# Sorting edges for a graph network: ranks by compare-and-sum over row counts in place of running counts in PSUM, and fewer message sources sent in the sort

## The chip, the cores and the metric

One core of a Trainium2 chip runs the whole program as one launch. The metric is device time in microseconds (us), median of the runs. The engines: PE multiplies matrices and writes PSUM, DVE does vector work, ACT functions, POOL memsets and index-driven (indirect) DMAs, SP the plain DMAs. They are ordered only by semaphores.

## The reference

Four graph layers over 50,000 nodes of 256 values and 25,000 edges (`src`, `dst`, types, weights), each with a residual sum and a layer norm around it: a weighted sum of neighbours with a product (mean layer), a relational layer in two parts, two attention hops, and an interaction layer.

```python
x = _layernorm(x + _L0_gnn_ref(x, ..., edge_weight, src, dst))
x = _layernorm(x + _L1_gnn_ref(x, edge_index, edge_type_16, ...))
x = _layernorm(x + _L2_gnn_ref(x, ..., edge_index, edge_type_24, 2))
x = _layernorm(x + _L3_gnn_ref(x, src, dst, edge_weight, ...))
# inside a layer, for example:
agg = jax.ops.segment_sum(edge_weight[:, None] * x[edge_col], edge_row, num_segments=x.shape[0])
out = jnp.concatenate([agg, x], axis=1) @ W.T
```

The sums over neighbours need the edges grouped by node. The kernel sorts them itself, at the start: that is the part which is changed.

## The kernel before

Nodes are cut into 391 tiles of 128. An item is a group of at most 128 edges whose node lies in one tile. `sort_edges` gives each edge a place in the item lists, once by `src` (o = 0) and once by `dst` (o = 1), and one in the list of messages by relation. Edges lie as 125 partitions by 200 columns (EP, EC). The bucket of an edge is its node's tile; its rank is the seed of its bucket (128 times the bucket's first item) plus the number of edges of the bucket that come before it.

The sort goes in this order on DVE (its queue is in order, and `Chain.step` waits for each instruction):
- keys, record fields, the message places (L489 to L530), then `passed_chunks` and `chunk_kind` (L532 to L536) and a signal `s_rec` (L537) on which POOL starts to send.
- the histogram (L548 to L551): for each column and order a one-hot [125, 392] (`make`, L544) that PE adds up over all partitions with the matrix of ones into `hist` (L608). Each column waits for the ring of 8 one-hots.
- from the counts the base, end and seed of each bucket (L553 to L561), the tables of the items (`Tables.make`, L361 to L391), which SP turns through memory.
- the ranks (L566 to L590): `rank[o]` in PSUM starts as the seeds. For each column PE adds to every partition the one-hots of the partitions before it (L616, `before`); DVE reads the rank of its own edge with one compare-and-sum (L576, key equal to iota, times `rank`, summed into `rank_f`); then PE adds the rest (L626, `not_before`), and goes on to the next column. Two orders take turns. After each four columns DVE makes item and lane numbers and places (L581 to L588), and signals `s_placed`.
- `tables.number` (L592), small.

POOL sends with indirect DMAs, each of one column of 125 records or sources (`Scatter.send`, L282): the first 80 columns of sources to the message list; then per four columns, when placed, four columns of records of order 0 and two of sources (L645 to L650). It waits for the landing of each twenty when it starts the next but one. The phase ends with a barrier of all engines; `combine_weights` follows, then `mean_layer`.

`mean_layer` runs over items, a pair at a time. POOL gathers the rows of both items (L208) into a ring of 8 slots, and may gather pair p when PE is through with pair p - 4 (L223). The first 192 pairs are unrolled on POOL, and `between(pair)` (L851 to L856) sends scatters behind the gathers: 6/5 a pair, the 200 columns of records of order 1 first, then the sources that the sort has left. PE sums the gathered rows with a one-hot (L931) and multiplies (L941, L944); DVE accumulates and normalizes (L873 to L895); ACT evaluates squares, roots and the result.

## Time and profile before

| | us |
|---|---|
| runs: median (lowest, highest) of 3 | 7257.34 (7241.2, 7273.64) |
| span of the profiled execution | 7237.5 |
| PE busy, share of the span | 6315.2 (87%) |
| DVE busy | 5168.2 (71%) |
| ACT busy | 4246.8 (59%) |
| POOL busy | 3966.9 (55%) |

The page gives the span of the profiled execution, from its first to its last instruction, and no other time of it; the span lies 3.7 us below the fastest run and 19.8 us below the median. The busy shares are means over phases that differ: the sort takes the first 696 us, with ACT idle and DVE nearly full; after it PE is the busiest. A line of the page's slices shows the same: DVE at 9, 8, 8, 7 tenths in the first four slices of 181 us, ACT at 0 for three.

### The profile page before, as it was taken

The numbers are of one execution on the slowest core, as the hardware profiler recorded it, in microseconds if no ns is written. First come the engines' busy times: TensorE is split into PE (matmuls) and PEld (weight loads), VectorE is DVE, ScalarE is ACT, GpSimd is POOL, SyncE is SP. The second block draws the span as 40 slices with busy tenths as digits, with TensorE's granted clock in tenths as the row PEclk, the third lists the DMA queues.
The fourth block names the chain that finished last, engine by engine and source line by source line (L and its number), as shares of the span: only waits on it lengthen the run. The fifth ranks groups of instructions, "written<-read, shape, count | busy, mean of one in ns | idle before, by whom it ended". The sixth has DMA issues, their size and how long they took to land. (4 is left out here: it accounts for less than half of the span.)

```text
span 7237.5 us, 161640 instructions
## 1 busy us (share of the span) xinstructions
PE 6315.2 (87%) x35080; PEld 5058.0 (70%) x35081; DVE 5168.2 (71%) x17621; ACT 4246.8 (59%) x14612; POOL 3966.9 (55%) x3682
## 2 busy tenths in 40 slices
PE   5676999997789997889999888887888888899999
PEld 2222788886687776679999766665766666788888
DVE  9887788887655554247777677776666666799998
ACT  0000888885214443138888566665677777677777
POOL 6676777775636666654444444444454444444444
PEclk9555999998879998999999899999898888999999
DMA  1201666666556665557777566665566666444444
GB/s 38 6 2 37 164 189 186 183 196 187 171 153 190 191 191 174 173 177 221 220 222 220 172 200 194 191 193 177 173 199 184 189 188 181 120 125 127 127 127 120
DMA packets 1165457, 1171.57 MB, mean 162 GB/s; under 512 B 308211, under 2 KB 1039755, under 8 KB 1164574
## 3 DMA queue, kind: packets, MB, share of 16 engines
q1 hardware_dynamic: 1007326, 953.22, 43.2%
q0 software_dynamic: 158016, 217.06, 12.7%
q8 instruction: 42, 0.69, 0.0%
q14 instruction: 73, 0.60, 0.0%
HBM read 961.54 MB, written 392.35 MB: 187 GB/s over the span
## 5 line engine op out<-in xcount | busy, mean ns | idle before, releaser
L208 POOL DMA_INDIRECT landing_first<-messages,by_dst_meta x768 | 837.3, 1090 | 723.7 <-PE l1b_ps_b L1481 363.6
L208 POOL DMA_INDIRECT landing_last<-x,by_dst_meta x384 | 438.4, 1142 | 555.9 <-PE l_ps_a L1618 483.1
L1926 POOL DMA_INDIRECT landing_last<-z,by_src_meta x408 | 416.8, 1021 | 578.6 <-PE l2b_ps_g L2225 422.2
L1926 POOL DMA_INDIRECT landing_last<-x,by_src_meta x408 | 419.1, 1027 | 487.8 <-PE l2a_ps_g L2225 283.9
L208 POOL DMA_INDIRECT landing_first<-in_x,by_src_meta x384 | 403.2, 1050 | 182.2 <-issue 89.2
L944 PE MATMUL l_ps_b<-l_w,l_agg_t 128*128 128x256 f32 x1624 | 423.0, 381 | 5.4 <-issue 5.3
L1479 PE MATMUL l1b_ps_b<-root,l1b_x_t 128*128 128x256 f32 x1600 | 426.1, 389 | 0.5
L1479 PE MATMUL l1a_ps_b<-root,l1a_x_t 128*128 128x256 f32 x1584 | 417.8, 386 | 8.3 <-issue 5.7
L941 PE MATMUL l_ps_b<-l_w,l_both 128*128 128x256 f32 x1624 | 422.4, 383 | 0.2 <-issue 0.2
L917 ACT ACT_TABLE_LOAD x1 | 1.3, 1283 | 705.2 <-PEq L117 705.2
L1435 ACT ACTIVATE l1a_x_t<-l1a_ps_x,by_dst_first 128x256 f32<-128x256 f32 x400 | 167.7, 470 | 415.0 <-PE l1a_ps_x L1467 317.5
L1637 PE MATMUL l_ps_b<-l_w,l_mix_t 128*128 128x256 f32 x1592 | 396.6, 392 | 13.8 <-issue 6.1
L1387 DVE SCALAR_TENSOR_TENSOR l1a_total<-l1a_total,by_dst_keep,l1a_ps_b 128x256 f32<-128x256 f32 x394 | 186.9, 474 | 289.5 <-PE l1a_ps_b L1481 222.6
L1633 PE MATMUL l_ps_b<-l_w,l_x_t 128*128 128x256 f32 x1592 | 382.8, 384 | 2.5 <-ACT l_x_t L1598 2.5
L626 PE MATMUL sort_ps_rank<-sort_onehot,not_before 125*125 125x392 bf16 x400 | 234.8, 587 | 166.3 <-DVE sort_junk L576 145.1
L1637 PEld LDWEIGHTS l_ps_b<-l_w,l_mix_t 128*128 128x128 f32 x1592 | 286.5, 190 | 120.5 <-DVE l_mix_t L1554 72.5
L944 PEld LDWEIGHTS l_ps_b<-l_w,l_agg_t 128*128 128x128 f32 x1624 | 310.4, 191 | 51.0 <-issue 8.8
L626 PEld LDWEIGHTS sort_ps_rank<-sort_onehot,not_before 125*125 125x125 bf16 x400 | 72.0, 180 | 388.7 <-DVE sort_junk L576 336.6
L1038 POOL DMA_INDIRECT landing_first<-x,rel_index x216 | 233.8, 1082 | 165.0 <-PE ma_ps_x L1160 81.0
L1479 PEld LDWEIGHTS l1a_ps_b<-root,l1a_x_t 128*128 128x128 f32 x1584 | 286.6, 191 | 52.6 <-issue 17.6
L705 PE MATMUL l2a_ps_g<-zero_row,ones_b 128*128 128x392 bf16 x1734 | 321.5, 330 | 0.0
L941 PEld LDWEIGHTS l_ps_b<-l_w,l_both 128*128 128x128 f32 x1624 | 295.3, 192 | 33.5
(391 smaller groups left out, 20404.9 us busy)
## 6 DMA issues: line engine op xcount, KB each, us to landing
l_both<-in_x_both SPq DMA_DIRECT2D x416, 256.0 KB
l2a_x<-x SPq DMA_DIRECT2D x53, 1216.0 KB
z<-l2a_result SPq DMA_DIRECT2D x400, 152.0 KB
x<-l1b_result SPq DMA_DIRECT2D x392, 152.0 KB
l2b_x<-z SPq DMA_DIRECT2D x53, 1024.0 KB
l1b_x<-h SPq DMA_DIRECT2D x408, 128.0 KB
l1b_res<-x SPq DMA_DIRECT2D x408, 128.0 KB
l2b_res<-x SPq DMA_DIRECT2D x51, 1024.0 KB
```

The source lines that it names most:

```text
L208: pool.indirect_dma_start(gathered[:, slot, 0:D], None, source[0:count, :], bass.IndirectOffsetOnAxis(ap=rows, axis=0), bounds_check=limit ...
L626: pe.matmul(rank[o][0:EP, :], c.not_before[0:EP, 0:EP], onehot[0:EP, o, k, :], start=False, stop=True, skip_group_check=True)
L705: pe.matmul(spare, c.ones_b[:], c.zero_row[:], start=True, stop=True)
L941: pe.matmul(ps_b[k % 4], x_t[:, m, i * P:(i + 1) * P], w[:, 2 + i, :], start=(i == 0), stop=False)
L944: last = pe.matmul(ps_b[k % 4], agg_t[:, k, i * P:(i + 1) * P], w[:, i, :], start=False, stop=(i == 1))
L1038: pool.indirect_dma_start(gathered[:, slot, :], None, x_in[0:N_NODES, :], bass.IndirectOffsetOnAxis(ap=relations.index[:, chunk:chunk + 1] ...
L1387: dve.scalar_tensor_tensor(total[:, k, :], total[:, (k - 1) % RING, :], graph.keep[:, bass.ds(j, 1)], ps_b[k // 2 % 2][:, k % 2, :], ALU.m ...
L1435: act.activation(x_t[:, k, :], ps_x[k // 2 % 2][:, k % 2, :], ACT.Copy, scale=graph.first[:, bass.ds(j, 1)]).then_inc(s["xt"], 1)
L1479: pe.matmul(sums, x_t[:, k, f * P:(f + 1) * P], root[:, f, :], start=(f == 0), stop=False)
L1633: pe.matmul(ps_b[k % 4], x_t[:, k, i * P:(i + 1) * P], w1[:, i, :], start=(i == 0), stop=False)
L1637: last = pe.matmul(ps_b[k % 4], mix_t[:, k, i * P:(i + 1) * P], w2[:, i, :], start=False, stop=(i == 1))
L1926: pool.indirect_dma_start(gathered[:, k, :], None, x_in[0:N_NODES, :], bass.IndirectOffsetOnAxis(ap=rows, axis=0), bounds_check=limit, oob ...
```

## The change

- Histogram: PE multiplies the one-hots by the identity in place of the matrix of ones, so `hist[o]` holds for each partition the counts of its own row. DVE copies them to SBUF (`row_counts`); PE makes the totals from them (`total`), for base, end and seed as before.
- Offsets: PE makes for each partition the counts of all partitions before it, plus the seeds, in `hist[o]`; DVE copies them to `values[:, o, 0:392]`. Behind them `values` holds ones.
- Ranks: `keys[:, o, :]` holds 0 to 391 and behind it the buckets of the 200 columns. The rank of column c is one instruction, `find_rank`: over 392 + c elements, key equal to the column's bucket, times `values`, summed. Offsets and the earlier columns of the own row come in one sum. PE has no part in it; the one-hots of the second pass, L616 and L626 are gone. The result goes to one of four junk tiles, and an instruction waits for the fourth before it. The columns are unrolled.
- Places: in parts, spread between the ranks of the following columns (`place_part`), each four columns as before.
- Order on DVE: `tables.make` goes behind column 127; `passed_chunks`, `chunk_kind` and `relations.kind` behind the last place.
- POOL: 100 columns of sources first, then one (not two) behind each four records, so 150 in the sort. The other 50 go to the mean layer, with 250 scatters over all 192 pairs.
- Tiles are laid over others that are no longer used (`spread`, `values`, `junk`).

The old second pass (L563, L566 to L590 on DVE, L610 to L628 on PE) is taken out; its code stands above.

```diff
-SOURCES_FIRST = 80
-SOURCES_BEFORE = SOURCES_FIRST + 2 * EC // (RING // 2)
+SOURCES_FIRST = 100
+SOURCES_BEFORE = SOURCES_FIRST + EC // (RING // 2)
+SCATTERS_LATER = 2 * EC - SOURCES_BEFORE
...
-    HALF = RING // 2
+    QUAD, WIDTH, JUNKS = RING // 2, TILES + 1, 4
+    FIRST_RANKS = 128
...
+        keys = ph.sb("keys", [EP, 2, WIDTH + EC], F32)
+        values = going_on[:].rearrange("p r c -> p (r c)")[:, 0:2 * (WIDTH + EC)].rearrange("p (o c) -> p o c", o=2)
+        junk = seen[:].rearrange("p r c -> p (r c)")[:, 0:JUNKS * (WIDTH + EC)].rearrange("p (o c) -> p o c", o=JUNKS)
+        row_counts = ph.sb("row_counts", [EP, 2, WIDTH], BF16)
+        rank_f = spread[0:EP, WIDTH:WIDTH + 2 * EC].rearrange("p (o c) -> p o c", o=2)
...
+                def find_buckets():
+                    with dve.Fori(0, EC // RING) as g:
+                        for k in range(RING):
+                            dve.wait_ge(s_hist, (g * RING + k) * 2 + 2)
+                            for o in range(2):
+                                at = dve.snap(g * RING + (o * (WIDTH + EC) + WIDTH + k))
+                                dve.tensor_scalar(onehot[0:EP, o, k, :], c.iota16[0:EP, :], flat(keys)[:, bass.ds(at, 1)],
+                                                  None, ALU.is_equal).then_inc(s_hot, 1)
+
+                def find_rank(column):
+
+                    for o in range(2):
+                        n = column * 2 + o
+                        if n >= JUNKS:
+                            dve.wait_ge(s_rank, n + 1 - JUNKS)
+                        width = WIDTH + column
+                        dve.scalar_tensor_tensor(junk[:, n % JUNKS, 0:width], keys[:, o, 0:width],
+                                                 keys[:, o, width:width + 1], values[:, o, 0:width], ALU.is_equal, ALU.mult,
+                                                 accum_out=rank_f[:, o, column:column + 1]).then_inc(s_rank, 1)
+
+                def place_part(quad, part):
+
+                    at = slice(quad * QUAD, (quad + 1) * QUAD)
+                    if part == 0:
+                        dve.wait_ge(s_rank, (quad + 1) * QUAD * 2)
+                        dve.tensor_copy(rank_i[:, :, at], rank_f[:, :, at]).then_inc(s_int, 1)
+                    elif part == 1:
+                        dve.wait_ge(s_int, quad + 1)
+                        dve.tensor_single_scalar(item_i[:, :, at], rank_i[:, :, at], 7, op=ALU.logical_shift_right)\
+                            .then_inc(s_split, 1)
+                        dve.tensor_single_scalar(lane_i[:, :, at], rank_i[:, :, at], P - 1, op=ALU.bitwise_and)\
+                            .then_inc(s_split, 1)
+                    else:
+                        dve.wait_ge(s_split, quad * 2 + 2)
+                        for o in range(2):
+                            dve.scalar_tensor_tensor(place[o][:, at], lane_i[:, o, at], float(ITEMS), item_i[:, o, at],
+                                                     ALU.mult, ALU.add).then_inc(s_placed, 1)
+
+                chain.step(dve.memset(values[:, :, WIDTH:], 1.0))
+                find_buckets()
+                dve.wait_ge(s_hist, 2 * (EC + RING))
+                for o in range(2):
+                    dve.tensor_copy(row_counts[:, o, :], hist[o][0:EP, :]).then_inc(s_counts, 1)
+                for o in range(2):
+                    b = graphs[o].buckets
+
+                    dve.wait_ge(s_total, o + 1)
+                    chain.step(dve.tensor_scalar(b["int"][:], total[o][:], float(P - 1), None, ALU.add))
+                    chain.step(dve.tensor_single_scalar(b["int2"][:], b["int"][:], 7, op=ALU.logical_shift_right))
+                    chain.step(dve.tensor_scalar(b["count"][:], b["int2"][:], 1.0, None, ALU.max))
+                    chain.step(dve.tensor_tensor_scan(b["end"][:], c.ones_row[:], b["count"][:], 0.0, ALU.mult, ALU.add))
+                    chain.step(dve.tensor_tensor(b["base"][:], b["end"][:], b["count"][:], ALU.subtract))
+                    dve.tensor_scalar(b["seed"][:], b["base"][:], float(P), None, ALU.mult).then_inc(s_start, 1)
+                for o in range(2):
+                    dve.wait_ge(s_offset, o + 1)
+                    dve.tensor_copy(values[:, o, 0:WIDTH], hist[o][0:EP, :]).then_inc(s_values, 1)
+                dve.wait_ge(s_values, 2)
+                for column in range(EC):
+                    find_rank(column)
+                    quad, part = column // QUAD - 1, column % QUAD
+                    if quad >= 0 and part < 3:
+                        place_part(quad, part)
+                    if column == FIRST_RANKS - 1:
+                        tables.make(dve, c, graphs, chain)
+                        dve.drain().then_inc(s_tab, 1)
+                for part in range(3):
+                    place_part(EC // QUAD - 1, part)
...
+                            pe.matmul(hist[o][0:EP, :], c.ident_b[0:EP, 0:EP], onehot[0:EP, o, k, :], start=False, stop=True,
                                       skip_group_check=True).then_inc(s_hist, 1)
                 for o in range(2):
+                    pe.wait_ge(s_counts, o + 1)
+                    pe.matmul(total[o][:], c.ones_b[0:EP, :], row_counts[:, o, :], start=True, stop=True).then_inc(s_total, 1)
                 for o in range(2):
+                    pe.matmul(hist[o][0:EP, :], c.before[0:EP, 0:EP], row_counts[:, o, :], start=True, stop=False)
+                    pe.wait_ge(s_start, o + 1)
+                    pe.matmul(hist[o][0:EP, :], c.ones[0:1, 0:EP], graphs[o].buckets["seed"][0:1, :], start=False, stop=True)\
+                        .then_inc(s_offset, 1)
...
-                for step in range(EC // HALF):
-                    pool.wait_ge(s_placed, 2 * step + 2)
-                    for q in range(HALF):
-                        records.send(step * HALF + q)
-                    for n in (2 * step, 2 * step + 1):
-                        sources.send(SOURCES_FIRST + n)
+                for quad in range(EC // QUAD):
+                    pool.wait_ge(s_placed, 2 * quad + 2)
+                    for q in range(QUAD):
+                        records.send(quad * QUAD + q)
+                    sources.send(SOURCES_FIRST + quad)
...
+    PAIRS_FIXED = TILES // RING * PAIRS
...
-                    for n in range(pair * 6 // 5, (pair + 1) * 6 // 5):
+                    for n in range(pair * SCATTERS_LATER // PAIRS_FIXED, (pair + 1) * SCATTERS_LATER // PAIRS_FIXED):
```

## Rows read from the trace of the kernel before

**Rows 1.** Stretch, length, busy us of PE, PEld, DVE, ACT, POOL, PEclk, DMA.
```profile
62.00:167.00 105.00, 97.77 (x399) 38.40 (x399) 104.85 (x399) 0.00 (x0) 84.63 (x67) 0.98 0.07 1
167.00:201.00 34.00, 4.34 (x9) 1.57 (x8) 30.82 (x101) 0.00 (x0) 17.77 (x14) 0.58 0.05 1
201.00:691.00 490.00, 337.10 (x800) 114.75 (x800) 413.95 (x1455) 0.00 (x0) 358.32 (x300) 0.50 0.14 3
...
705.00:1643.00 938.00, 870.46 (x4501) 744.85 (x4502) 773.62 (x3151) 809.15 (x2953) 687.38 (x611) 0.98 0.67 185
```

**Rows 2.** Groups by line, POOL, 210 to 691 us: count, busy, mean, idle.
```profile
L282 POOL DMA_INDIRECT item_records<-sort_rec,sort_place x200 | 240.1, 1200 | 113.5 <-DVE dst_place L588 67.8 <-issue 45.7
L282 POOL DMA_INDIRECT rel_source_rows<-rel_source,rel_place x100 | 118.6, 1186 | 30.5 <-issue 30.5
```

**Rows 3.** Timeline of POOL in the sort: start, us, instruction, idle before.
```profile
62.25 1.44 POOL L282 DMA_INDIRECT rel_source_rows<-rel_source,rel_place  x1 [44.95 <-DVEq L537]
...
168.03 1.24 POOL L282 DMA_INDIRECT rel_source_rows<-rel_source,rel_place  x1 [0.30 <-issue]
...
209.74 1.29 POOL L282 DMA_INDIRECT item_records<-sort_rec,sort_place  x1 [21.00 <-DVE dst_place L588]
...
682.71 1.19 POOL L282 DMA_INDIRECT item_records<-sort_rec,sort_place  x1 [0.70 <-DVE dst_place L588]
...
690.17 1.18 POOL L282 DMA_INDIRECT rel_source_rows<-rel_source,rel_place  x1 [0.30 <-issue]
```

**Rows 4.** Timeline of DVE in the ranks: start us, us, instruction.
```profile
480.66 0.17 DVE L581 CAST sort_rank_i<-sort_rank_f 125x8 int32<-125x8 f32 x1
...
481.51 0.32 DVE L544 TENSOR_SCALAR sort_onehot<-iota,sort_bucket 125x392 bf16<-125x392 f16 x1
...
483.98 0.61 DVE L576 SCALAR_TENSOR_TENSOR sort_junk<-iota,sort_bucket,sort_ps_rank 125x392 f32<-125x392 f32 x1
...
484.73 0.62 DVE L576 SCALAR_TENSOR_TENSOR sort_junk<-iota,sort_bucket,sort_ps_rank 125x392 f32<-125x392 f32 x1
```

**Rows 5.** POOL beside the tables, 174 to 190 us; groups of L373 and L890.
```profile
L282 POOL DMA_INDIRECT rel_source_rows<-rel_source,rel_place x10 | 13.3, 1326 | 3.0 <-issue 3.0
...
174.91 1.18 POOL L282 DMA_INDIRECT rel_source_rows<-rel_source,rel_place  x1 [0.30 <-issue]
...
187.55 1.19 POOL L282 DMA_INDIRECT rel_source_rows<-rel_source,rel_place  x1 [0.30 <-issue]
...
L373 DVE SCALAR_TENSOR_TENSOR sort_table_junk<-iota,sort_tile_id,src_base 128x391 f32<-128x391 f32 x5 | 3.1, 626 | 0.2
...
L890 DVE SCALAR_TENSOR_TENSOR l_shifted<-l_scaled,l_inner_scale,beta 128x256 f32<-128x256 f32 x346 | 150.9, 476 | 0.0
```

**Rows 6.** Groups of DVE by line, 0 to 1300 us: the chunk kinds.
```profile
L535 DVE TENSOR_REDUCE sort_chunk_kind<-sort_passed_chunks 1x216 f32<-1x3456 f32 x1 | 3.7, 3741 | 0.0
L532 DVE TENSOR_TENSOR sort_passed_chunks<-sort_last_chunk,iota 1x3456 f32<-1x3456 f32 x1 | 3.7, 3740 | 0.0
```

**Rows 7.** Timeline of POOL in the mean layer: first gathers of some pairs.
```profile
902.67 1.04 POOL L208 DMA_INDIRECT landing_first<-in_x,by_src_meta  x1 [1.06 <-remote]
...
921.25 1.01 POOL L208 DMA_INDIRECT landing_first<-in_x,by_src_meta  x1 [1.25 <-remote]
...
926.92 1.04 POOL L208 DMA_INDIRECT landing_first<-in_x,by_src_meta  x1 [0.30 <-issue]
...
945.65 1.02 POOL L208 DMA_INDIRECT landing_first<-in_x,by_src_meta  x1 [0.30 <-issue]
...
952.11 1.04 POOL L208 DMA_INDIRECT landing_first<-in_x,by_src_meta  x1 [0.95 <-remote]
```

**Rows 8.** Timeline of PE in the mean layer, no scatters: two pairs apart.
```profile
1659.84 1.05 PE L931 MATMUL l_ps_a<-l_hot,landing_first 128*128 128x128 f32 x8
...
1668.53 1.05 PE L931 MATMUL l_ps_a<-l_hot,landing_first 128*128 128x128 f32 x8
```

**Rows 9.** Waits, 720 to 1610 us: us in total, times, longest us.
```profile
POOL landing_first L208 <- remote: 79.1, 85, 1.3
```

More of the change, by code:

```diff
@@ L350, with __init__ @@
     KEEP = 3
-    def __init__(self, ph):
+    def __init__(self, ph, junk):
         self.ints = ph.sb("ints", [P, 2, 3, ITEM_CHUNKS], I32)
@@ L457, in sort_edges @@
         s_hot, s_hist, s_start = ph.sem("hot"), ph.sem("hist"), ph.sem("start")
-        s_hot2, s_rank, s_read, s_empty = ph.sem("hot2"), ph.sem("rank"), ph.sem("read"), ph.sem("empty")
+        s_counts, s_total, s_offset, s_values = (ph.sem(n) for n in ("counts", "total", "offset", "values"))
+        s_rank, s_empty = ph.sem("rank"), ph.sem("empty")
         s_int, s_split, s_placed = ph.sem("int"), ph.sem("split"), ph.sem("placed")
@@ L462, in sort_edges @@
         s_out, s_rel = ([ph.pool_dma_sem(f"{n}{k}") for k in range(2)] for n in ("out", "rel"))
-        tables = Tables(ph)
+        tables = Tables(ph, spread)
         def flat(t):
@@ L536, in _ @@
                 dve.tensor_scalar(relations.kind[:], chunk_kind[:], float(R1 - 1), None, ALU.min)
-                dve.drain().then_inc(s_rec, 1)
-                dve.wait_ge(s_keys, 2)
-                def make(column, k, sem):
-                    for o in range(2):
-                        a = dve.snap(column + o * (EC + 1)) if not isinstance(column, int) else column + o * (EC + 1)
-                        dve.tensor_scalar(onehot[0:EP, o, k, :], c.iota16[0:EP, :], flat(bucket)[:, bass.ds(a, 1)], None,
-                                          ALU.is_equal).then_inc(sem, 1)
@@ L548, in _ @@
-                with dve.Fori(0, EC // RING) as g:
-                    for k in range(RING):
-                        dve.wait_ge(s_hist, (g * RING + k) * 2 + 2)
-                        make(g * RING + k, k, s_hot)
-                dve.wait_ge(s_hist, 2 * (EC + RING))
-                for o in range(2):
-                    b = graphs[o].buckets
-                    chain.step(dve.tensor_scalar(b["int"][:], hist[o][:], float(P - 1), None, ALU.add))
-                    chain.step(dve.tensor_single_scalar(b["int2"][:], b["int"][:], 7, op=ALU.logical_shift_right))
-                    chain.step(dve.tensor_scalar(b["count"][:], b["int2"][:], 1.0, None, ALU.max))
-                    chain.step(dve.tensor_tensor_scan(b["end"][:], c.ones_row[:], b["count"][:], 0.0, ALU.mult, ALU.add))
-                    chain.step(dve.tensor_tensor(b["base"][:], b["end"][:], b["count"][:], ALU.subtract))
-                    chain.step(dve.tensor_scalar(b["seed"][:], b["base"][:], float(P), None, ALU.mult))
```

79 lines of the change are left out of this document (17 added, 62 removed).

## The prediction

> **What bounds the kernel now.** I read the stages first: busy time of each engine stretch by stretch [rows 1]. The sort lies alone in front of everything: until its barrier no other phase runs, so each microsecond it ends earlier moves the whole rest forward. It has three stretches: the histogram (62 to 167 us, DVE 104.85 us busy of 105), the tables (167 to 201) and the ranks (201 to 691, DVE 414 and POOL 358 us busy of 490). Then comes the mean layer with its scatters (705 to about 1610), and after that nothing that the change touches.
>
> Second, who ends the ranks. POOL's groups [rows 2] and its single starts [rows 3]: after the histogram it sends, for each four columns, four records and two sources. Its waits for `dst_place` are 67.8 us in 50, of which 21.00 are the first; the steps start at 209.74 (the first) and 682.71 (the fiftieth), so one step takes 472.97 / 49 = 9.65 us. Six DMAs at 1.20 + 0.30 us are 8.97. So the ranks are bound by DVE by 0.7 us a step, with POOL close behind: whatever DVE gains above 7% is worth nothing unless POOL's list also gets shorter. This is the key to the change, for it does both.
>
> Third, the mean layer, where the taken-away sources go: there POOL issues two gathers and one or two scatters a pair, and the time of a pair depends on how many [rows 7].
>
> **Sort: DVE's side.** Before, a column costs two one-hots (L544) and two reads (L576, 0.62 us), which hand over to PE and back through semaphores [rows 4]. The change drops the second pass of one-hots, all 400 matmuls of L626 and 400 of L616, and the waits between. What is left per column is two compare-and-sum instructions from SBUF, 392 elements wide at column 0 and 591 at column 199. The trace shows the same form from SBUF in L373: 0.62 us for 391 elements, and L890 takes 476 ns for 256 [rows 5]; that is (626 - 476) / 135 = 1.11 ns an element, so the added mean width of 99.5 elements is 0.11 us. Two L576 start 0.75 us apart with their waits [rows 4]. The least that two starts can lie apart I take as 0.55 us for 392 elements, 0.626 less the 0.08 that reading an accumulator takes beside it (an estimate). So one costs 0.66 us with no wait between and 0.86 with all of them; I take 0.75, since the new one waits only for the fourth before it. 400 of them are 300 us (264 to 344). The five instructions that split ranks and make places stay; in one step they run from 480.66 to 481.51 [rows 4], 0.85 us, so 43 us; the tables, moved behind column 127, are some 25 of the 30.8 us that DVE is busy in their stretch [rows 1]. DVE then needs about 370 us for the ranks (332 to 412), where it has 490 now.
>
> Before that come small new things: a memset and the copies of row counts, two matmuls of totals, two pairs of offset matmuls and two copies, some 5 us by my estimate, all while POOL is still sending its first hundred sources. The histogram's matmul against the identity instead of the ones is the same size, and DVE paces it anyway (104.85 of 105 us busy): nothing. Moved out of the way: `passed_chunks` and its reduction, 3.74 + 3.74 us [rows 6] with the clamp behind them 7.8 us; they stood ahead of the signal that starts POOL, and go to the end of DVE's list, where POOL still has sources and records to send. That is a clean 7.8 us.
>
> **Sort: POOL's side, which sets the end.** POOL starts at 62.25 - 7.8 = 54.45. It has 100 + 50 sources and 200 records, 350 DMAs in place of 380. During the histogram it starts one each (168.03 - 62.25) / 67 = 1.58 us [rows 3], so 67 are gone by 160.1, when the histogram ends. 283 are left. Their period is the unknown: in the ranks of before it is 1.49 (1.19 + 0.30, [rows 2]); beside L373, two thirds of DVE's work there, it is (187.55 - 174.91) / 8 = 1.58, and by the group of ten that reaches into that stretch 1.33 + 0.30 = 1.63 [rows 5]. In the new ranks nearly every DVE instruction is of L373's form, but POOL has its index reads in both. I take 1.55, between the two: 438.7 us, so the last DMA ends at 598.8 and not at 691.35 (690.17 + 1.18): 92.6 us earlier. With 1.49 it is 108, with 1.63 it is 70.
>
> Does DVE keep ahead? It starts ranks at about 172 us and has the first four columns placed at 184; POOL has sent its hundred sources at about 211, so DVE leads by 27 us. A step takes POOL 5 x 1.55 = 7.75 us. DVE's takes 0.85 us and eight instructions, whose width grows by 64 elements on average in the first 128 columns and by 163 in the rest: 5.8 to 7.4 us, then 6.7 to 8.3. So the lead grows by 11 to 62 us in the first 32 steps, the tables take 25, and the last 18 steps lie between -10 and +19. Even with all the worse ends it is 27 + 11 - 25 - 10 = 3 us: POOL never waits after its first hundred sources. The waits of 67.8 us go, and what is late next is POOL's own issuing.
>
> **Mean layer.** Before, 20 sources and the 200 records of the other order lie in the mean layer, 220 scatters, at 6/5 a pair over the first 184 of 192 pairs (148 with one, 36 with two, 8 with none). After, it is 50 + 200 = 250, over all 192 (134 with one, 58 with two). What a pair costs: 902.67 to 952.11 is ten pairs, of which those that start at 921.25 and at 945.65 have two scatters and take 5.67 and 6.46, mean 6.07; the other eight take (49.44 - 12.13) / 8 = 4.66 [rows 7]. Pairs without scatters take (1668.53 - 1659.84) / 2 = 4.35 [rows 8]. Before: 148 x 4.66 + 36 x 6.07 + 8 x 4.35 = 943.0. After: 134 x 4.66 + 58 x 6.07 = 976.5. So +33.5 us. Bounds: if POOL's waits there, 79.1 us in 85 [rows 9], took up the extra scatters, only the last 8 pairs would pay, +2; at 1.6 us for each extra scatter, the 1.5 that one takes in the ranks [rows 2] and a little for the gathers beside it, it is +38. I take the value of the rows, since in them a second scatter is not absorbed although POOL waits about 1 us in every second pair: the waits come back right behind it. The landing of the sources is needed only in the phase after, and the last of them goes out at pair 191, before the layer's last pairs.
>
> PE's clock is no term: it is 0.50 of full (1.2 GHz) all through the ranks [rows 1], with PE waiting, and nothing there is bound by it.
>
> **Sum.** -92.6 + 33.5 = -59 us. The profiled execution has a span of 7237.5 us; the median of the runs, 7257.3, is 20 us above it and the fastest 4 above. Nearly all the change lies in stretches with the same pace in every execution, so I take it off the median: 7198 us, 0.8% less.
>
> **Rivals.**
> The waits absorb the scatters (chance 0.13): for it speaks that POOL is at times 1 us early; against it that two-scatter pairs still cost 1.4 us more. -92.6 + 2: 7167 us.
>
> POOL is held by DVE's port (0.07), the one that ends slower. Where a DMA's issue must wait for a whole compare-and-sum, its period becomes 1.49 + 0.62 = 2.11 us; 283 of them are 597 us, the sort ends at 757, 66 later than before, and with the mean layer it is +99: 7357 us. Break-even is a period of 1.76, slower by 0.5% is 1.89. For it: the mean of 1.33 us beside L373 against 1.19. Against it: the first and the last DMA of that stretch take 1.18 and 1.19 us all the same, though L373 and its like run back to back there [rows 5]. The Trainium skill has this rule (SBUF — State Buffer, Who interferes with whom): a Vector instruction with two SBUF inputs takes its second through the read interface that GpSimd shares, exclusive for the whole instruction, against GpSimd instructions that read SBUF. By that rule L576 of before, with one input in PSUM, was harmless and the new one is not; the trace agrees in part, with 0.09 to 0.14 us a DMA and not 0.62.
>
> The mean layer pays more than its pairs show (0.07): with two-scatter pairs every 3.3 pairs POOL can lose its lead of four pairs, and PE waits for rows. At 5.3 us a pair the layer's 192 pairs are 1018 us, +75: 7240 us, no difference.
>
> DVE stays the bound of the ranks (0.06): the 400 waits and the unrolled list of columns cost more, 0.97 us an instruction. From 0.9 on DVE loses its lead. 172 + 50 x 8.6 + 25 + 7 = 634: -57 + 33.5: 7234 us. Something else, the change not doing what it says among it: 0.01.
>
> **Numbers.** The forecast has 0.66. Its own ends are 7257 - 108 + 2 = 7151 and 7257 - 70 + 38 = 7225; with the spread of medians and the two rivals near them, 7145 to 7235. A change under 0.5% (36 us) can't be told from none. Faster: 0.64 of the forecast, the absorbed case and half of the DVE case, 0.80; within: 0.14; slower: 0.06.
>
> **What would show it.** After: the first source at 54 us; L576's place taken by an instruction of 0.6 to 0.8 us without PE; POOL's waits for `dst_place` near nothing after the first hundred sources; the period of its DMAs 1.55; the phase after the sort at about 604 us and not 696; in the mean layer 58 pairs of 6.1 and 134 of 4.7 us, and the layer 33 us longer from its first gather to its last pair. It is wrong if the period is above 1.65, or if the layer grows by more than 40 or less than 20 us.

## The result and the profile after

The changed kernel takes 7207.24 us in the median of 5 runs (7199.59 to 7214.92), the kernel before 7257.34 in 5 runs beside it; the ratio is 0.9935, 95% interval 0.9917 to 0.9954. That is 50 us or 0.7% less. The interval excludes no difference; its near end, 0.46%, lies just under the 0.5% that the prediction asks of a faster kernel. Forecast were 7198 us, 59 less. The profiled execution has a span of 7205.5 us.

I read the same views in the same order. First the stretches (windows view; the columns are those of [rows 1]):

```profile
54.00:160.00 106.00, 100.46 (x399) 54.26 (x399) 105.41 (x401) 0.00 (x0) 84.85 (x67) 0.97 0.07 1
160.00:200.00 40.00, 5.30 (x11) 1.67 (x10) 37.87 (x137) 0.00 (x0) 32.69 (x25) 0.55 0.07 1
200.00:600.00 400.00, 0.00 (x0) 0.00 (x0) 286.79 (x1024) 0.00 (x0) 322.15 (x252) 0.50 0.23 4
620.00:1640.00 1020.00, 918.44 (x4749) 788.12 (x4749) 816.95 (x3324) 852.87 (x3114) 768.85 (x672) 0.98 0.64 179
```

The histogram is as it was (DVE 105.41 us busy of 106). In the ranks PE has nothing to do; DVE is busy for 287 of 400 us and POOL for 322. POOL's 0.30 us ahead of each of its 252 DMAs fill the remaining 76: it is never waiting. So the bound has gone from DVE, waiting with PE, to POOL's issuing. POOL's timeline in the sort and at the turn to the mean layer (start, us, instruction, idle time before; for [rows 3]):

```profile
55.02 1.38 POOL L283 DMA_INDIRECT rel_source_rows<-rel_source,rel_place  x1 [37.70 <-issue]
...
299.33 1.19 POOL L283 DMA_INDIRECT rel_source_rows<-rel_source,rel_place  x1 [0.30 <-issue]
300.82 1.19 POOL L283 DMA_INDIRECT item_records<-sort_rec,sort_place  x1 [0.30 <-issue]
302.32 1.66 POOL L283 DMA_INDIRECT item_records<-sort_rec,sort_place  x1 [0.30 <-issue]
304.28 1.19 POOL L283 DMA_INDIRECT item_records<-sort_rec,sort_place  x1 [0.30 <-issue]
...
610.98 1.19 POOL L283 DMA_INDIRECT rel_source_rows<-rel_source,rel_place  x1 [0.30 <-issue]
...
628.29 1.06 POOL L209 DMA_INDIRECT landing_first<-in_x,by_src_meta  x1 [1.65 <-issue]
```

The first source starts at 55.02 and not 62.25; the last DMA of the sort ends at 612.17 and not 691.35. Among them are DMAs of 1.66 us between others of 1.19, the mark of something that holds POOL. One is held far longer, at the end of the ranks. Here it is with its two successors, and below them what DVE does at the time:

```profile
478.56 4.12 POOL L283 DMA_INDIRECT item_records<-sort_rec,sort_place  x1 [0.31 <-issue]
482.99 1.19 POOL L283 DMA_INDIRECT rel_source_rows<-rel_source,rel_place  x1 [0.30 <-issue]
484.48 1.19 POOL L283 DMA_INDIRECT item_records<-sort_rec,sort_place  x1 [0.30 <-issue]
...
477.88 3.74 DVE L608 TENSOR_TENSOR sort_passed_chunks<-sort_last_chunk,iota 1x3456 f32<-1x3456 f32 x1
481.65 3.74 DVE L611 TENSOR_REDUCE sort_chunk_kind<-sort_passed_chunks 1x216 f32<-1x3456 f32 x1
```

Beside the instruction with two SBUF tensors (`passed_chunks`, to 481.62) the DMA takes 2.93 us more and ends 1.06 us after it; beside the equally long reduction with one, two DMAs take their 1.19. POOL's groups over all the ranks (for [rows 2]) have no wait for `dst_place` left:

```profile
L283 POOL DMA_INDIRECT item_records<-sort_rec,sort_place x200 | 256.8, 1284 | 62.3 <-issue 62.3
```

DVE's timeline (start, us, instruction): the first, the middle and the last compare-and-sums. They run back to back, 0.55 us apart at 392 elements, 0.65 at 491 and 0.75 at 591, and the place steps between them cost 0.08 us an instruction:

```profile
171.35 0.63 DVE L557 SCALAR_TENSOR_TENSOR sort_seen<-sort_keys,sort_going_on 125x392 f32<-125x392 f32 x1
...
171.91 0.62 DVE L557 SCALAR_TENSOR_TENSOR sort_seen<-sort_keys,sort_going_on 125x392 f32<-125x392 f32 x1
...
299.25 0.15 DVE L576 SCALAR_TENSOR_TENSOR sort_place<-sort_lane_i,sort_item_i 125x4 int32<-125x4 int32 x1
299.33 0.20 DVE L576 SCALAR_TENSOR_TENSOR dst_place<-sort_lane_i,sort_item_i 125x4 int32<-125x4 int32 x1
299.45 0.72 DVE L557 SCALAR_TENSOR_TENSOR sort_seen<-sort_keys,sort_going_on 125x491 f32<-125x491 f32 x1
...
300.10 0.72 DVE L557 SCALAR_TENSOR_TENSOR sort_seen<-sort_keys,sort_going_on 125x491 f32<-125x491 f32 x1
...
475.62 0.82 DVE L557 SCALAR_TENSOR_TENSOR sort_seen<-sort_keys,sort_going_on 125x591 f32<-125x591 f32 x1
...
476.37 0.83 DVE L557 SCALAR_TENSOR_TENSOR sort_seen<-sort_keys,sort_going_on 125x591 f32<-125x591 f32 x1
```

The mean layer ends with the last `l_scaled`. Here the row of that tile before and after (duration min/median/max in ns, first and last start in us):

```profile
L885 DVE SCALAR_TENSOR_TENSOR l_scaled<-l_products,l_inner_minus_mean,gamma x402: 467/476/527, 740.8 to 1711.5; 128x256 f32<-128x256 f32 x134
```

```profile
L896 DVE SCALAR_TENSOR_TENSOR l_scaled<-l_products,l_inner_minus_mean,gamma x402: 468/477/532, 660.7 to 1665.2; 128x256 f32<-128x256 f32 x134
```

I take "the layer" from its first gather to the last start of `l_scaled`. Before it is 1711.5 - 708.41 = 1003.1 us, after 1665.2 - 628.29 = 1036.9. The first gather of before:

```profile
708.41 1.05 POOL L208 DMA_INDIRECT landing_first<-in_x,by_src_meta  x1 [1.66 <-issue]
```

The balance of the change is thus -80.1 us up to the first gather, +33.8 in the layer, -46.3 at its end, against -50 between the medians. The two spans differ by 32 only: in this one pair of executions the phases behind the layer, which the change doesn't touch, ran 14 us longer, less than the 42 us by which the runs of before differ among themselves. It did not come again in the second pair of traces, of the same two kernels: behind the layer they differ there by 3 us.

### The profile page after: what moved, and what is told of

It reads as the page before. It is cut to its first block and busy times, and to the rows that moved or that the text cites. A ratio compares the mean times of both kernels' runs of the same rounds, so it can differ in the third digit from the quotient of the medians.

```text
span 7205.5 us, 158095 instructions
## 1 busy us (share of the span) xinstructions
PE 5992.7 (83%) x34282; PEld 4956.2 (69%) x34283; DVE 5044.5 (70%) x17224; ACT 4251.2 (59%) x14612; POOL 4017.7 (56%) x3682
## 5 line engine op out<-in xcount | busy, mean ns | idle before, releaser
L884 DVE SCALAR_TENSOR_TENSOR l_agg_t<-l_agg_t,by_src_keep,l_ps_a 128x256 f32<-128x256 f32 x410 | 195.8, 478 | 188.5 <-remote 153.7
L942 PE MATMUL l_ps_a<-l_hot,landing_first 128*128 128x128 f32 x1640 | 247.2, 289 | 93.2 <-DVE l_hot L673 47.3
```

The costliest lines, as they stand in the source:

```text
L884: dve.scalar_tensor_tensor(agg_t[:, k, :], agg_t[:, (k - 1) % RING, :], graph.keep[:, bass.ds(j, 1)], ps_a[k % 2], ALU.mult, ALU.add)\
L942: last = pe.matmul(ps_a[k % 2][:, f * P:(f + 1) * P], gathered[:, k, f * P:(f + 1) * P], hot[:, k, :], start=True, stop=True)
```

## The experiments

They ran on other chips, where both kernels are 4 to 5% faster; so each has its ratio to the kernel before on the same chip (6911 to 6919 us), and its inner times are compared with kernels run there. The changed kernel itself stands first, then the kernel before.

**The changed kernel again.** 

> The changed kernel, unaltered, to stand on the same chip as the runs beside it. Expected: a ratio of 0.993 to the kernel before, as on the first chip; last DMA of the sort at about 612 us, 250 scatters and 192 pairs in 966 us if this chip is like the first, in about 924 if it is like the second.

6879.80 us, ratio 0.9945 (0.9928 to 0.9962); the ratios in brackets are 95% intervals throughout. The sort's last DMA ends at 610.38, the layer takes 1617.1 - 626.52 = 990.6 us. A pair with one scatter takes 4.34 us here (4.62 on the first chip), one with two 6.04 (6.09). In three other runs with this same layer it takes 986.4, 987.1 and 995.2 us, so a difference of 5 us between two layers says nothing.

**The kernel before again.** 

> The kernel before, unaltered, for a trace of it on a chip of the kind of the last ten runs. Theory A (the change's effect lies in the sort and the mean layer alone): last DMA of the sort at about 691 us as in the first trace, its mean layer of 192 pairs and 220 scatters takes the same 877 us as that of the rewritten ranks with the old split. Theory B (its mean layer is slower for another reason, such as what lies where in SBUF): over 885 us, which would be the part of the gain that the sort does not account for.

6918.59 us against 6918.73, ratio 0.9999 (0.9990 to 1.0009): two sets of runs of one kernel agree to 0.1%. First the start of its layer and its last `l_scaled`, then the start in the changed kernel on this sort of chip:

```profile
705.06 1.06 POOL L208 DMA_INDIRECT landing_first<-in_x,by_src_meta  x1 [1.65 <-issue]
...
L885 DVE SCALAR_TENSOR_TENSOR l_scaled<-l_products,l_inner_minus_mean,gamma x402: 468/476/544, 730.4 to 1659.3; 128x256 f32<-128x256 f32 x134
```

```profile
626.52 1.06 POOL L209 DMA_INDIRECT landing_first<-in_x,by_src_meta  x1 [1.65 <-issue]
...
L896 DVE SCALAR_TENSOR_TENSOR l_scaled<-l_products,l_inner_minus_mean,gamma x402: 469/476/525, 651.8 to 1617.1; 128x256 f32<-128x256 f32 x134
```

Its layer takes 954.2 us. So here the change is worth -78.5 us to the first gather and +36.4 in the layer, together -42, with medians 39 apart. Both terms are close to those of the first chip (-80.1 and +33.8). The gathers of 192 pairs spread over 883.4 us, between the two theories (877 and over 885); the next run shows why the layer itself is longer than that of the old split with new ranks.

**One part alone: the rewritten ranks, with two sources behind each four records and 20 left to the mean layer, as before.** Run twice.

```diff
-SOURCES_FIRST = 100
-SOURCES_BEFORE = SOURCES_FIRST + EC // (RING // 2)
+SOURCES_FIRST = 80
+SOURCES_BEFORE = SOURCES_FIRST + 2 * EC // (RING // 2)
...
-                    sources.send(SOURCES_FIRST + quad)
+                    for n in (2 * quad, 2 * quad + 1):
+                        sources.send(SOURCES_FIRST + n)
```

> The changed kernel with the old split of the sources: 80 first, two behind each four record lists, 20 in the mean layer. Theory (POOL's list alone ends the sort, a second scatter costs a pair of the mean layer 1.45 us): the last DMA of the sort ends about 46 us later than in the changed kernel (30 more at 1.5 to 1.6 us, so near 658 us), the 192 pairs take 35 us less, in all 7207 + 11 = 7218 us. Rival (DVE ends the sort too, or the mean layer's waits absorb the scatters): the sort ends less than 20 us later, or the pairs get less than 10 us shorter; then 7180 or 7245 us.

> The rewritten ranks with the old split of the sources once more, beside the kernel before on the same chip. Theory A: last DMA of the sort 32 us earlier than in the kernel before, the mean layer the same within 4 us, so 32 us shorter as a whole, a ratio of 0.9954. Theory B: the first time measured, a ratio of 0.9927 or 50 us, comes again, and the traces show in which phase the other 18 us lie.

6872.85 us and 6873.78, ratios 0.9927 (0.9902 to 0.9952) and 0.9937 (0.9919 to 0.9954). That is as much as the whole change gives. The second run's rows:

```profile
658.41 1.19 POOL L283 DMA_INDIRECT rel_source_rows<-rel_source,rel_place  x1 [0.30 <-issue]
...
676.59 1.06 POOL L209 DMA_INDIRECT landing_first<-in_x,by_src_meta  x1 [1.65 <-issue]
...
L897 DVE SCALAR_TENSOR_TENSOR l_scaled<-l_products,l_inner_minus_mean,gamma x402: 467/476/525, 701.6 to 1615.4; 128x256 f32<-128x256 f32 x134
```

The first gather is 28.5 us earlier than in the kernel before, and the layer, 938.8 us (940.9 in the first run), is 15.4 us shorter though it has the same 220 scatters. Theory A, the 32 us of the sort alone, was wrong for the whole; theory B held, and the rest lies in the layer. The new rule of dealing them spreads the 220 over all 192 pairs, so that 28 have two; the old one put them in 184, and 36 had two. On these chips a pair with one scatter (4.34 to 4.37 us) costs no more than a pair with none; those stand at the end of the kernel before, 4.35 us apart on PE here as in [rows 8]:

```profile
1634.70 1.05 PE L931 MATMUL l_ps_a<-l_hot,landing_first 128*128 128x128 f32 x8
1639.04 1.05 PE L931 MATMUL l_ps_a<-l_hot,landing_first 128*128 128x128 f32 x8
```

So only second scatters cost: 8 fewer of them at the 1.7 us by which a pair with two is longer are 13.6 of the 15.4 us.

Against the changed kernel: its sort ends 49.2 us earlier (610.38 against 659.60) and its layer is 51.8 longer. Moving 30 sources into the mean layer is worth nothing.

**The other part alone: the sources moved as in the change, ranks as before.**

```diff
-SOURCES_FIRST = 80
-SOURCES_BEFORE = SOURCES_FIRST + 2 * EC // (RING // 2)
+SOURCES_FIRST = 100
+SOURCES_BEFORE = SOURCES_FIRST + EC // (RING // 2)
+SCATTERS_LATER = 2 * EC - SOURCES_BEFORE
...
-                    for n in (2 * step, 2 * step + 1):
-                        sources.send(SOURCES_FIRST + n)
+                    sources.send(SOURCES_FIRST + step)
...
-                    for n in range(pair * 6 // 5, (pair + 1) * 6 // 5):
+                    for n in range(pair * SCATTERS_LATER // PAIRS_FIXED, (pair + 1) * SCATTERS_LATER // PAIRS_FIXED):
```

> The kernel before with the new split of the sources alone. Theory (there DVE ends the ranks): the last DMA of the sort ends within 3 us of 691 us although POOL has 30 fewer; POOL's waits for places grow from 68 to about 110 us; the mean layer's pairs take 35 us more; 7257 + 33 = 7290 us. Rival (POOL ended the ranks all along): the sort gets 45 us shorter and the whole 7247 us.

6943.04 us, ratio 1.0043 (1.0026 to 1.0059): slower by a difference that is clear of noise, if under the prediction's 0.5%. With a shorter list POOL only waits longer for DVE. Its group of records between 210 and 680 us has 98.8 us of waits for `dst_place` where [rows 2] has 67.8:

```profile
L283 POOL DMA_INDIRECT item_records<-sort_rec,sort_place x200 | 239.6, 1198 | 145.7 <-DVE dst_place L589 98.8 <-issue 46.9
```

The first gather starts at 695.28, 9.8 us earlier than in the kernel before; the layer takes 991.3 us, 37.1 more; together +27, measured +31 between the medians. So the shorter list gave 9.8 us and neither nothing, as a list fully hidden behind DVE would have, nor the 45 us of its 30 DMAs. They come from DVE: without POOL's sixth DMA in a step its two integer splits are shorter. The first of them in the kernel before and here (215 to 665 us); the second falls from 348 to 179 ns:

```profile
L583 DVE TENSOR_SCALAR sort_item_i<-sort_rank_i 125x8 int32<-125x8 int32 x47 | 18.2, 387 | 1.6
```

```profile
L584 DVE TENSOR_SCALAR sort_item_i<-sort_rank_i 125x8 int32<-125x8 int32 x48 | 9.1, 189 | 1.6
```

DVE's step falls from 9.58 to 9.41 us, 8.5 us over 49 steps. That the sixth DMA held the splits is argued from this difference alone.

**Is DVE off the path? Each compare-and-sum waits for the one before.**

```diff
-                        if n >= JUNKS:
-                            dve.wait_ge(s_rank, n + 1 - JUNKS)
+                        if n:
+                            dve.wait_ge(s_rank, n)
```

> The changed kernel, but each compare-and-sum of the ranks waits for the one just before it, not for the fourth before it; all the work stays. Theory A (POOL's own issuing sets the end of the ranks, DVE is far ahead): DVE's spacing grows from 0.6 to about 0.8 us and its ranks end some 60 to 80 us later (about 540 to 560 us, still ahead of the places that POOL needs), and the time stays within 6 us of the changed kernel; POOL's period in the ranks may even fall, from 1.6 towards 1.55, because DVE's instructions fill less of the time. Theory B (DVE bounds the ranks): the end of the sort moves by what DVE's ranks lose, 60 us or more, and POOL shows waits for the places.

6873.85 us, ratio 0.9935 (0.9919 to 0.9952), not slower than the changed kernel's 6879.80. The last compare-and-sum starts at 509.19, in the changed kernel on this chip at 476.21:

```profile
508.32 0.83 DVE L557 SCALAR_TENSOR_TENSOR sort_seen<-sort_keys,sort_going_on 125x591 f32<-125x591 f32 x1
...
509.19 0.83 DVE L557 SCALAR_TENSOR_TENSOR sort_seen<-sort_keys,sort_going_on 125x591 f32<-125x591 f32 x1
```

The full wait costs 0.12 us an instruction (0.87 against 0.75) where no place step fills it, 33 us in all and not the 60 to 80 I expected, and the sort ends at the same place: the last DMA starts at 609.32, against 609.20. At its end DVE is 100 us ahead of POOL's last DMA. POOL's period fell from 1.68 to 1.54 us between 171 and 320 us, rose from 1.54 to 1.65 between 345 and 478, and stayed higher until DVE's ranks were over; the parts cancel. So a little more room between DVE's instructions may free POOL or hold it more.

**What holds POOL? The values of the compare-and-sum in PSUM, so that one of its two tensors comes from SBUF.** PE writes the offsets there itself, so DVE's two copies fall away too.

```diff
-        values = going_on[:].rearrange("p r c -> p (r c)")[:, 0:2 * (WIDTH + EC)].rearrange("p (o c) -> p o c", o=2)
+        values = [ph.ps(f"values{o}", [P, 4 * D]) for o in range(2)]
...
-                                                 keys[:, o, width:width + 1], values[:, o, 0:width], ALU.is_equal, ALU.mult,
+                                                 keys[:, o, width:width + 1], values[o][0:EP, 0:width], ALU.is_equal, ALU.mult,
```

> The changed kernel with the values (offsets and ones) of the compare-and-sum left in PSUM, so that this instruction has one SBUF tensor input and not two; same widths, same count. Theory A (the second SBUF input holds POOL): POOL's period during the ranks falls from 1.68 (171 to 320 us) and 1.56 (345 to 478) to 1.49 to 1.52 us, the sort ends 18 to 25 us earlier, 7185 us. Theory B (the short copies and integer steps of the places hold POOL): the period stays at 1.6 and the time within 4 us of the changed kernel.

6845.01 us, ratio 0.9894 (0.9859 to 0.9929). POOL's groups between 171 and 320 us, in the changed kernel (on the first chip; here the means are the same, 1.38 us) and in this one:

```profile
L283 POOL DMA_INDIRECT item_records<-sort_rec,sort_place x50 | 69.4, 1387 | 15.2 <-issue 15.2
L283 POOL DMA_INDIRECT rel_source_rows<-rel_source,rel_place x39 | 53.4, 1370 | 11.9 <-issue 11.9
```

```profile
L283 POOL DMA_INDIRECT item_records<-sort_rec,sort_place x59 | 70.0, 1186 | 18.0 <-issue 17.4 <-DVE dst_place L576 0.6
L283 POOL DMA_INDIRECT rel_source_rows<-rel_source,rel_place x41 | 48.6, 1186 | 12.5 <-issue 12.5
```

A DMA takes 1.186 us and not 1.38, with none over 1.25 us where 58% were, beside DVE instructions of the same width and the same 0.72 us. The period falls from 1.68 to 1.49 us, and the last DMA ends at 588.82, 21.6 us before that of the changed kernel on these chips. So what lengthened POOL's issue was the second SBUF tensor of DVE's instruction, and nothing about DVE being busy.

The price is no constant. POOL's records in the changed kernel between 250 and 270 and between 370 and 390 us, with DVE busy for all 20 us of both:

```profile
L283 POOL DMA_INDIRECT item_records<-sort_rec,sort_place x10 | 14.9, 1494 | 3.0 <-issue 3.0
L283 POOL DMA_INDIRECT item_records<-sort_rec,sort_place x11 | 13.1, 1192 | 3.4 <-issue 3.4
```

The instruction is the same but for its width (0.69 and 0.76 us on average); it costs a record's DMA 0.3 us in one stretch and nothing in the other. With the values in PSUM both stretches have 1.18 to 1.19. How the two engines' beats fall together seems to decide it; that is argued, not shown.

**The same in the mean layer: the scale and shift vectors in PSUM.**

```diff
+        ps_gb = ph.ps("gb", [P, 2 * D])
...
-                                                 gamma[:], ALU.add, ALU.mult).then_inc(s["scaled"], 1)
+                                                 ps_gb[:, 0:D], ALU.add, ALU.mult).then_inc(s["scaled"], 1)
...
-                        dve.scalar_tensor_tensor(shifted[:, k, :], scaled[:, k, :], inner.scale[:, k:k + 1], beta[:],
+                        dve.scalar_tensor_tensor(shifted[:, k, :], scaled[:, k, :], inner.scale[:, k:k + 1], ps_gb[:, D:2 * D],
...
+                dve.tensor_copy(ps_gb[:, 0:D], gamma[:]).then_inc(s["gb"], 1)
+                dve.tensor_copy(ps_gb[:, D:2 * D], beta[:]).then_inc(s["gb"], 1)
```

> The changed kernel, but in the mean layer the scale and shift vectors lie in PSUM, so that the layer's scalar_tensor_tensor instructions read one tensor less from SBUF. Theory A (the port between DVE and POOL that lengthened POOL's DMAs in the ranks lengthens them in the mean layer too): the scatters' and gathers' mean duration on POOL falls by 0.03 to 0.1 us, and the 192 pairs, 4 or 5 DMAs each, take 15 to 50 us less. Theory B (the pairs are bound elsewhere, by POOL's waits for the other cores' or engines' releases and by PE): durations fall a little or not at all and the pairs take the same within 8 us.

6850.30 us, ratio 0.9897 (0.9880 to 0.9913). POOL's groups between 640 and 1500 us, first the changed kernel's on the same chip:

```profile
L209 POOL DMA_INDIRECT landing_first<-in_x,by_src_meta x355 | 380.8, 1073 | 108.2 <-issue 102.4 <-PE l_ps_a L942 5.8
L283 POOL DMA_INDIRECT item_records<-dst_records,dst_place x197 | 256.4, 1302 | 60.3 <-issue 60.3
```

```profile
L209 POOL DMA_INDIRECT landing_first<-in_x,by_src_meta x365 | 380.9, 1044 | 111.2 <-issue 107.6 <-PE l_ps_a L946 3.7
L283 POOL DMA_INDIRECT item_records<-dst_records,dst_place x197 | 243.7, 1237 | 60.3 <-issue 60.3
```

250 x 0.065 + 384 x 0.029 = 27 us less of issuing, and the layer is 28.2 us shorter (962.4 against 990.6): nearly all of POOL's time there lies on the path. DVE's two instructions became 5 ns shorter as well (476 to 471), 4 us over the layer; DVE waits 116 us for `l_ps_a` there, so that explains little of the gain.

**50 sources left out of the mean layer.** This kernel doesn't send the last 50 sources, to price the scatters.

> The changed kernel with the mean layer's last 50 scatters left out (message sources of 50 columns are never written, so those messages are missing from the relational layer): 200 scatters over 192 pairs, 184 with one and 8 with two. Theory (1.45 us for each second scatter): first to last gather of the 192 pairs 899 us against 966 to 971, in all 7207 - 70 = 7137 us. Rival (the pair is held by something other than POOL's issue and only reacts to scatters on average): a gain in proportion to the mean rate of 0.26 a pair, (4.35 to 5.06 us a pair for 1.30), 27 us, 7180 us.

6787.63 us, ratio 0.9812 (0.9780 to 0.9844). The layer takes 909.2 us with 8 pairs of two, 938.8 with 28, 990.6 with 58: 1.5 us for each second scatter in the first step, 1.7 in the other. The 50 scatters are worth 81 us, near the theory's 70 and far from the rival's 27. In these three every pair has at least one scatter, so scatters and pairs of two rise together, by 20 and by 30; what tells them apart is the kernel before, with 220 scatters, 36 pairs of two and 954.2 us.

**Is a lone second scatter partly absorbed? The 58 pairs with two come first.**

```diff
+                def sent_by(pair):
+                    return pair + min(pair, SCATTERS_LATER - PAIRS_FIXED)
...
-                    for n in range(pair * SCATTERS_LATER // PAIRS_FIXED, (pair + 1) * SCATTERS_LATER // PAIRS_FIXED):
+                    for n in range(sent_by(pair), sent_by(pair + 1)):
```

> The changed kernel, but the 250 scatters of the mean layer are dealt otherwise over its 192 pairs: the first 58 pairs take two each, the other 134 one each, in place of two at every third or fourth pair. Theory A (a second scatter lengthens its own pair by its issue time, nothing is absorbed by POOL's lead): the sum over the pairs is the same, the layer within 6 us of the changed kernel's, 58 pairs of about 6.0 us in a row and then 134 of 4.35. Theory B (POOL's lead of four pairs absorbs part of a lone second scatter, so bunching costs more): the pairs with two go to 6.5 us or more and the layer is over 15 us longer. Theory C (POOL's waits cost something behind each lone double, so bunching saves): over 10 us shorter.

6867.83 us, ratio 0.9937 (0.9920 to 0.9955). 58 pairs of 5.93 us in a row, then pairs of 4.41; the layer is 2.4 us longer than the changed kernel's, within the spread. The order neither absorbs nor loses anything that can be seen.

**An earlier start beside the values in PSUM, and then all three edits.**

```diff
-                    dve.tensor_copy(rec[o][:, :, OTHER].bitcast(I32), raw[:, 1 - o, :])
-                    dve.tensor_copy(rec[o][:, :, NODE], local_i[:, o, :])
...
                 dve.drain().then_inc(s_rec, 1)
...
+                    dve.tensor_copy(rec[o][:, :, OTHER].bitcast(I32), raw[:, 1 - o, :])
+                    dve.tensor_copy(rec[o][:, :, NODE], local_i[:, o, :])
```

The buckets and the keys move behind the signal in the same way.

> The run with the values of the ranks in PSUM, and beside it an earlier start of POOL: the copies that fill the fields of the records (all but the kind) move from ahead of the signal that lets POOL send its first source to behind it. Theory A (in the sort each microsecond of POOL's list counts, whatever DVE does): the first source starts at about 50 us and not at 55.0, the last DMA of the sort ends at about 584, 28 us before that of the changed kernel, and the time is 28 us shorter than that of the changed kernel on the same chip, 0.4%. Rival (the start is bound by the keys' arrival, or the moved copies delay the histogram, which POOL doesn't wait for until its hundredth source): 23 us, the value of the run before, and no more.

> The run with values in PSUM and the early start, together with the mean layer's scale and shift vectors in PSUM: both ports' edits at once. Theory A (each takes its POOL time out of its own stretch, and both stretches lie on the path): last DMA of the sort at about 584 us as in the one, 192 pairs 26 to 28 us shorter than in the changed kernel as in the other; together 50 to 56 us shorter than the changed kernel on the same chip, so a ratio of 0.986 to 0.987 to the kernel before. Rival (with the sort earlier something of the mean layer, such as the inputs or the clock, comes late, and part is given back): 30 us or less, 0.990.

The first: 6849.83 us, ratio 0.9894 (0.9877 to 0.9911); the first gather starts at 597.85, 28.7 us before the changed kernel's, 7.1 of them from the start. Its layer (995.2 us) is 8 us longer than that of the values in PSUM alone (987.1), so nothing is left of the 7. Its median is not below that of the values in PSUM alone; such 7 us, 0.1%, are below what the intervals can tell.

All three: 6810.49 us, ratio 0.9850 (0.9836 to 0.9864), the fastest of the kernels that compute everything, 1.5% below the kernel before and about 1% below the changed one by the ratio of the two ratios. The layer and the sort give what the single runs gave; 50 to 56 us were expected and the traces show 58.5. POOL starts at 48.44, and the turn to the layer is here:

```profile
48.44 1.38 POOL L283 DMA_INDIRECT rel_source_rows<-rel_source,rel_place  x1 [31.09 <-issue]
...
580.57 1.18 POOL L283 DMA_INDIRECT rel_source_rows<-rel_source,rel_place  x1 [0.30 <-issue]
...
597.57 1.05 POOL L209 DMA_INDIRECT landing_first<-in_x,by_src_meta  x1 [1.66 <-issue]
```

The sort is 29.0 us shorter than the changed kernel's, the layer (961.0) 29.6: the gains add up.

## Why the prediction came out near, step by step

- **The start**: 54.45 forecast, 55.02 measured. Right; `passed_chunks` and its reduction now run at 477.88, where POOL has 133 us of DMAs before it. But they were called a clean 7.8 us: at their new place `passed_chunks` holds one DMA of POOL for 2.93 us, which the sum had at nothing.
- **DVE's ranks**: about 370 us forecast, 332 to 412; measured from 171.35 to 477.95, 307 us, outside that range. The instruction was taken at 0.75 us, and 0.55 to 0.75 by width is true, mean 0.65; the place steps were taken at 43 us and take some 20. I had bounded it by no wait and a full wait and stood between them, since it waits for the fourth before it; such a wait costs nothing, as the spacing shows. It moved nothing, since DVE was ahead anyway.
- **The bound passes to POOL**: right. No wait for the places is in the trace, and 33 us more of DVE changed nothing.
- **POOL's period after the histogram**: 1.55 forecast, (612.17 - 160.1) / 283 = 1.597 measured. This is the mis-sized term: 283 x 0.047 = 13 us, so the sort gave 79.2 us and not 92.6. The rows beside L373 had said 1.58 and 1.63 [rows 5]; I discounted them towards the period of before, because two single DMAs there were short. The averages were the evidence: DMAs untouched at 1.19 stand between others held at up to 1.68, so two short ones say nothing. By stretches the period was 1.68 from 171 to 320 us, 1.56 from 345 to 478 and 1.49 from 491 on. Above 1.19 us each, the DMAs have 17 us in the first of them, 4 in the second and 4 in the three beside `passed_chunks` and the numbering of the tables.
- **The port as a rival**: its mechanism is shown, its price was wrong. The rule of the Trainium skill (SBUF — State Buffer, Who interferes with whom), that a Vector instruction with two SBUF inputs keeps GpSimd's reads out, agrees with the run with the values in PSUM: 1.38 us became 1.186. That a held DMA waits for the end of the instruction agrees too: beside `passed_chunks` it ended 1.06 or 1.07 us after it in three runs (the changed kernel, the values in PSUM, the old split), whether it had started 0.68, 0.71 or 1.31 us into it. But the rival charged each DMA the whole 0.62 us of a compare-and-sum. A DMA waits at most for what is left of the one in flight, and many find the port free: the mean price was 0.19 us from 171 to 320 us and 0.05 from 345 to 478. Which part of the 1.19 us reads the indices is open; no run takes the issue apart.
- **The mean layer**: +33.5 forecast, +33.8 measured on the first chip and +36.4 on the others. Right, and for its reason: 58 pairs of two and 134 of one. The rivals fall with it: no absorption (1.5 to 1.7 us a second scatter), and no loss of lead (58 pairs of two in a row cost 5.93 us each). On the other chips a pair with one scatter cost 0.3 us less than the rows said; that moved the rise little, because their number falls only from 148 to 134.
- **The sum**: -59 forecast, -46.3 in the traces, -50 in the medians. What was off is the size of POOL's period, 1.55 for 1.597 us; the path and the mean layer's price held. (At a period of 1.49 the sort's gain is 110 us and not the 108 that I wrote; no chance rested on it.)
- **What I said of the parts was wrong**, though no number rested on it. I wrote that what DVE gains above 7% is worth nothing unless POOL's list gets shorter too, and that the change doing both was the key. For the end of the sort that held (28.5 us earlier with the old list, 78.5 with the short one), but not for the kernel. The ranks alone give 0.9927 and 0.9937, the moved sources alone 1.0043, both together 0.9945. The shorter list gave the sort 49 us and cost the layer 52: the same DMAs at the same price in two places. The comparison to make was 30 x 1.55 us saved in the sort against the 33.5 us paid in the layer, and the 13 us between them lay in the 8 last pairs without a scatter, which the old split of the sources could use as well (28 pairs of two and not 36).

What stays open: why a pair of one scatter takes 4.62 us on the first chip, where POOL waits for a release in some 80 of the 192 pairs (61.7 us in the changed kernel), and 4.34 on the others, where its waits in the layer come to 5.8 us; and why the two spans of the first pair of traces drifted 14 us apart behind the layer. Also open: why the same compare-and-sum holds a DMA for 0.3 us in one stretch and for nothing in another.

## What to carry to other kernels

Before moving work from one stretch to another, price the same instruction in both: if its engine sets the end in each, the move gains nothing, and it hides which part of a change earned the time. When one engine is taken off the path, look at the next one's period beside the new instructions, and take the mean of the group, not single rows. An instruction moved beside another engine's list must be priced there as well. Where POOL issues indirect DMAs on the path, give DVE's long instructions at most one SBUF tensor and put the other, a constant row or a prefix, in PSUM: three such instructions gave 50 us here.

## What the runs showed of the hardware

- A compare-and-sum with its accumulator read costs 0.55 us at 392 elements and 0.75 at 591 when nothing waits, about 1.0 ns an element, and 0.12 us more when each waits for the one before (0.87 at 591).
- With one operand in PSUM it is as long as with both in SBUF (717 ns against 722 in the median); only POOL notices: 1.19 against 1.38 us for an indirect DMA's issue from 171 to 320 us.
- One DVE instruction of 3.74 us with two SBUF tensors made an indirect DMA of 1.19 us take 4.12; one of 3.74 us with a single one left two at 1.19.
- A DVE copy of 784 elements beside POOL's memsets took 10.29 us at the very start:

```profile
7.46 10.29 DVE L495 COPY sort_keys<-iota 125x784 f32<-125x784 f32 x1 [5.02 <-PEq L118]
17.66 0.24 DVE L498 TENSOR_SCALAR sort_bucket_i<-sort_raw 125x200 int32<-125x200 int32 x1
```

It cost 0.5 us (the next instruction but one starts at 17.94, in the kernel before at 17.45), most of what the first source came late by. It was no more because there too the first instruction, of 200 elements, took 3.73 us, where its like took 0.26 right after, and ended at 17.42. In both kernels POOL's memsets run from 7.4 to 17.3 us beside it. That they held DVE is argued from this, not shown by a run without them.
